# A graph attention layer on one core: four stages in place of five, head sums spread over six steps, and another order of the last steps

## The reference

```python
h = x @ W                                       # x: 8192 x 128
e = (h @ a1)[:, None] + (h @ a2)[None, :]
e = jnp.where(e > 0, e, 0.2 * e)
e = jnp.where(adj > 0, e, -9e15)                # adj: 8192 x 8192 int32, a one in 4096
attention = jax.nn.softmax(e, axis=1)
out = layernorm(x + elu(attention @ h))
```

## Time and profile before

| | us |
|---|---|
| median of 3 runs | 720.44 |
| lowest and highest | 719.63, 721.66 |
| the profiled execution | 721.3 |
| its span, first to last instruction | 719.5 |
| TensorE busy with products in it | 557.4 (77%) |
| ScalarE busy | 520.5 (72%) |
| VectorE busy | 480.7 (67%) |
| GpSimd busy | 443.6 (62%) |
| 285.57 MB moved, mean rate | 397 GB/s |

### The profile page before, as it was taken

One profiled execution on the slowest core, in us unless ns is written; L12 is line 12 of the kernel. 1 busy time (PEld: TensorE's weight loads), 2 busy tenths in 40 slices (PEclk: granted clock), 3 DMA queues, 4 the chain that ended last, 5 costly groups with the idle time before them and its releaser, 6 DMA issues.

```text
span 719.5 us, 11920 instructions
## 1 busy us (share of the span) xinstructions
PE 557.4 (77%) x3071; PEld 351.2 (49%) x3071; DVE 480.7 (67%) x2051; ACT 520.5 (72%) x414; POOL 443.6 (62%) x668
## 2 busy tenths in 40 slices
PE   0858799987778887778888787887778787777884
PEld 0323455554455554555455554554455554544583
DVE  1474777767766667667667667677766667667565
ACT  0847578787878777887878787878878777878511
POOL 2016267766766676676667676667666766777741
PEclk9987798899999999998889999799999999999957
DMA  9999999999999999999999999999999999999901
GB/s 353 326 422 422 384 413 429 427 422 425 428 425 429 426 426 429 425 427 425 428 426 427 427 428 427 428 426 426 428 425 428 429 427 428 426 423 424 284 17 31
DMA packets 34582, 285.57 MB, mean 397 GB/s; under 512 B 5512, under 2 KB 13856, under 8 KB 18048
## 3 DMA queue, kind: packets, MB, share of 16 engines
q1 hardware_dynamic: 29008, 276.83, 92.1%
q0 software_dynamic: 5120, 8.42, 3.3%
q10 hardware_dynamic: 432, 0.07, 0.1%
HBM read 283.18 MB, written 4.19 MB: 399 GB/s over the span
## 4 chain that ended last, share of the span: by engine, by line
DMA 63%; PE 12%; ACT 10%; DVE 6%; issue 5%; POOL 2%; SPq 0%; ACTq 0%; POOLq 0%; DVEq 0%
DMA adj_sb<-in_adj 60%; ACT adj_squared L551 10%; PE fold L653 7%; DMA a_sb<-in_L_gnn_a 2%; PE misc L678 2%; PE fold L649 1%; POOL edge_row L362 1%; PE x_att_ps L701 1%; DMA nb<-in_x,index 1%; DVE s_all L838 1%; PE small L668 1%; DVE x_times_wa L836 1%; DVE top_map L852 0%; DVE spread L374 0%; POOL nb L497 0%
## 5 line engine op out<-in xcount | busy, mean ns | idle before, releaser
L551 ACT ACTIVATE adj_squared<-adj_sb 128x4096 bf16<-128x4096 int32 x128 | 462.4, 3613 | 103.2 <-DMA adj_sb<-in_adj 97.2
L653 PE MATMUL fold<-adj_sb,bit_ident 128*128 128x512 bf16 x1024 | 302.0, 445 | 0.0
L497 POOL DMA_INDIRECT nb<-in_x,index x160 | 165.7, 1036 | 92.4 <-issue 64.2
L653 PEld LDWEIGHTS fold<-adj_sb,bit_ident 128*128 128x128 bf16 x1024 | 109.4, 107 | 150.6 <-issue 61.0
L649 PE MATMUL fold<-col_no,ident_bf 128*128 128x512 bf16 x128 | 53.2, 416 | 114.2 <-DMA adj_sb<-in_adj 101.7
L852 DVE MAX8 top_map<-fold 128x8 f32<-128x512 f32 x128 | 89.5, 699 | 67.1 <-PE fold L653 62.4
L362 POOL TENSOR_SCALAR edge_row<-row_iota,edge_in 128x128 f32<-128x128 int32 x186 | 129.4, 710 | 0.0
L378 POOL TENSOR_TENSOR spread<-edge_row,edge_w 128x384 f32<-128x384 f32 x60 | 51.9, 885 | 66.4 <-DVE edge_w L965 66.3
L477 POOL TENSOR_SCALAR empty_diag<-ident,counts 128x128 f32<-128x128 f32 x64 | 42.2, 665 | 68.5 <-DVE counts L889 35.4
L649 PEld LDWEIGHTS fold<-col_no,ident_bf 128*128 128x128 bf16 x128 | 16.4, 128 | 129.1 <-issue 101.4
L701 PEld LDWEIGHTS x_att_ps<-spread,nb 128*128 128x128 f32 x372 | 58.6, 225 | 9.8 <-issue 4.7
(11 more groups left out here) (120 smaller groups left out, 623.4 us busy)
## 6 DMA issues: line engine op xcount, KB each, us to landing
adj_sb<-in_adj SPq DMA_DIRECT2D x127, 2048.0 KB, 15.9
out<-x_sb SPq DMA_DIRECT2D x2, 1536.0 KB
nb<-in_x,index POOLq DMA_INDIRECT x160
adj_sb<-in_adj SPq DMA_DIRECT2D x2, 1024.0 KB, 15.1
out<-x_sb SPq DMA_DIRECT2D x5, 128.0 KB
out<-x_sb SPq DMA_DIRECT2D x1, 384.0 KB
W_sb<-in_L_gnn_W ACTq DMA_DIRECT2D x1, 64.0 KB, 7.9
x_sb<-in_x SPq DMA_DIRECT2D x4, 0.5 KB, 17.7
```

Source lines behind the costliest of these rows:

```text
L497: nc.gpsimd.indirect_dma_start(out=nb_of(j, g)[:, c, :], out_offset=None, in_=x[:, :], in_offset=bass.IndirectOffsetOnAxis(ap=index[:, g, ...
L551: nc.scalar.activation(adj_squared[:, h % 2, :], adj_sb[:, h % LOAD_SLOTS, :], ACT.Square, accum_out=half_sum[:, h:h + 1]).then_inc(square ...
L653: last = nc.tensor.matmul(fold[:, h % LOAD_SLOTS, :], bit_ident[:, b, :], adj_low[:, h % LOAD_SLOTS, b * FOLD:(b + 1) * FOLD, 0], start=Fa ...
```

## The change

The arithmetic is the same. On each engine work is written in another order:

- VectorE: `finish` is done for p3, behind `weights`, in place of p4 at the head of the step; `pick` of the first half comes ahead of `route`; `edge_weights` comes ahead of `lists` (except in the last step); in `lists` the count goes ahead of the cap.
- ScalarE: `copy_sums` comes behind the first square, `scale` (now for p4) behind the second, then `exp_weights` and `exp_elu`, all ahead of the third and fourth square.
- TensorE: `sum_neighbours` comes behind the first fold, ahead of `count_starts`; `times_W` ahead of the third fold.
- The head sums are made in eighths: four in step (0, 0), none in (0, 1), one in each of the four steps after that. TensorE's row sums are spread over three steps.
- The ending: VectorE does final's `indices` ahead of back1's `neighbour_scores`, and has no `finish(back3)` there, since that is now in the last step; ScalarE has no `scale(back4)` there. Final's five gathers have a semaphore each, for which its dot products wait one by one. SP waits for all five before its first store. Final's `sum_neighbours` starts when the spread of the first of its two tiles is done (`first_spread`).

The diff, whole but for a few lines of context:

```diff
         adj_sb = sb("adj_sb", [P, LOAD_SLOTS, HALF], i32)
         adj_low = adj_sb[:].bitcast(bf16).rearrange("p s (c two) -> p s c two", two=2)
         adj_squared = sb("adj_squared", [P, 2, HALF], bf16)
-        x_times_wa = sb("x_times_wa", [P, TILES // 4, D], fp32)
+        x_times_wa = sb("x_times_wa", [P, TILES // 8, D], fp32)
         ident = sb("ident", [P, P], fp32)
         bit_ident = sb("bit_ident", [P, BITS, P], bf16)
         ident_bf = sb("ident_bf", [P, P], bf16)
...
         weights_loaded = sem("weights_loaded")
         loaded = [sem(f"loaded{s}") for s in range(LOAD_SLOTS)]
         rest_loaded = sem("rest_loaded")
+        chunk_gathered = [sem(f"chunk_gathered{c}") for c in range(CHUNKS)]
+        first_spread = sem("first_spread")
         gathered = [sem(f"gathered{g}") for g in range(GROUPS)]
         out_stored = sem("out_stored")
         x_again = sem("x_again")
...
                     if eng is nc.vector:
                         last_one = eng.tensor_scalar(spread[:, t, k, :], edge_row[:, g, t, k, :], edge_w[:, c:c + 1],
                                                      None, ALU.mult)
+                if is_final(j, g) and t == 0:
+                    last_one.then_inc(first_spread, 1)
                 if eng is nc.gpsimd:
                     mine = edge_w[:, SPANS[t][0]:SPANS[t][0] + SPAN]
                     last_one = eng.tensor_tensor(spread[:, t, :, :], edge_row[:, g, t, :, :],
...
                 step(*back1)
                 step(*final)
+                for landed in chunk_gathered:
+                    sp.wait_ge(landed, 16)
                 for lo, hi in STORES:
                     sp.wait_ge(scaled, hi)
                     nc.sync.dma_start(out_tiles[:, lo * PAIR:hi * PAIR, :], x_sb[:, lo * PAIR:hi * PAIR, :]
...
                         nc.gpsimd.indirect_dma_start(
                             out=nb_of(j, g)[:, c, :], out_offset=None, in_=x[:, :],
                             in_offset=bass.IndirectOffsetOnAxis(ap=index[:, g, c:c + 1], axis=0),
-                            bounds_check=N - 1, oob_is_err=False).then_inc(gathered[g], 16)
+                            bounds_check=N - 1, oob_is_err=False).then_inc(
+                                chunk_gathered[c] if is_final(j, g) else gathered[g], 16)
                 def step(i, g):
                     p1, p2, p4 = (stage(i, g, k) for k in (1, 2, 4))
...
                     last.then_inc(scaled, 1)
                 def step(i, g):
-                    now, p2, p3, p5 = (stage(i, g, k) for k in (0, 2, 3, 5))
-                    if p5:
-                        scale(*p5)
+                    now, p2, p3, p4 = (stage(i, g, k) for k in (0, 2, 3, 4))
                     square_half(*now, 0)
-                    square_half(*now, 1)
-                    square_half(*now, 2)
                     if p3:
                         copy_sums(*p3)
+                    square_half(*now, 1)
+                    if p4:
+                        scale(*p4)
                     if p2:
                         exp_weights(*p2)
-                    square_half(*now, 3)
                     if p3:
                         exp_elu(*p3)
+                    square_half(*now, 2)
+                    square_half(*now, 3)
                 steps(act, step)
                 step(*back1)
                 step(*final)
-                scale(*back4)
                 exp_weights(*back1)
                 copy_sums(*back2)
                 exp_elu(*back2)
...
                 def sum_neighbours(j, g):
-                    pe.wait_ge(spread_ready, count(j, g))
+                    if is_final(j, g):
+                        pe.wait_ge(first_spread, 1)
+                    else:
+                        pe.wait_ge(spread_ready, count(j, g))
                     pe.wait_ge(diag_made, count(j, g))
                     if first(j) and g == 0:
                         pe.wait_ge(x_mean_ready, 1)
                     elif not is_final(j, g):
                         pe.wait_ge(x_att_ready, count(j, g) - 1)
                     for t in range(PAIR):
+                        if is_final(j, g) and t == 1:
+                            pe.wait_ge(spread_ready, count(j, g))
                         for k, c in enumerate(SPANS[t]):
                             nc.tensor.matmul(x_att_of(j, g)[:, t, 0:P], nb_of(j, g)[:, c, :], spread[:, t, k, :],
                                              start=k == 0, stop=False)
...
                 def step(i, g):
                     now, p1, p2, p3 = (stage(i, g, k) for k in range(4))
                     fold_half(*now, 0)
+                    if p3:
+                        sum_neighbours(*p3)
                     if p1:
                         count_starts(*p1)
                     fold_half(*now, 1)
-                    if p3:
-                        sum_neighbours(*p3)
                     if p1:
                         fill_edges(*p1)
                     if p2:
                         send_scores(*p2)
+                    if p3:
+                        times_W(*p3)
                     fold_half(*now, 2)
                     fold_half(*now, 3)
-                    if p3:
-                        times_W(*p3)
                     if p2:
                         send_shares(*p2)
-                    if first(i):
-                        sum_rows(g * TILES // GROUPS, (g + 1) * TILES // GROUPS)
+                    if first(i) and g == 0:
+                        sum_rows(0, TILES // 2)
+                    if first(i) and g == 1:
+                        sum_rows(TILES // 2, 3 * TILES // 4)
+                    if isinstance(i, int) and (i, g) == (1, 0):
+                        sum_rows(3 * TILES // 4, TILES)
                 def keep_warm(products, bank=3):
...
                 dve.wait_ge(wa_made, 1)
                 s.after(nc.vector.tensor_copy(wa_bc[:].rearrange("p k c -> p (k c)"), misc[:, P:3 * P]))
-                quarter = TILES // 4
+                eighth = TILES // 8
                 def own_scores(q):
-                    dve.wait_ge(x_loaded[q], 16)
-                    v.after(nc.vector.tensor_tensor(x_times_wa[:], x_sb[:, q * quarter:(q + 1) * quarter, :],
-                                                    wa_bc[:, 1:2, :].to_broadcast([P, quarter, D]), ALU.mult))
-                    v.after(nc.vector.reduce_sum(s_all[:, q * quarter:(q + 1) * quarter], x_times_wa[:], AX.X))
+                    dve.wait_ge(x_loaded[q // 2], 16)
+                    v.after(nc.vector.tensor_tensor(x_times_wa[:], x_sb[:, q * eighth:(q + 1) * eighth, :],
+                                                    wa_bc[:, 1:2, :].to_broadcast([P, eighth, D]), ALU.mult))
+                    v.after(nc.vector.reduce_sum(s_all[:, q * eighth:(q + 1) * eighth], x_times_wa[:], AX.X))
                 def mean_row():
                     dve.wait_ge(x_summed, 1)
...
                         dve.wait_ge(diag_made, count(j, g) - 1)
                         dve.wait_ge(tallied, count(j, g) - 1)
                     v.after(nc.vector.tensor_scalar(is_code[:], sent[:, :, 0:SLOTS], float(NO_CODE), None, ALU.is_gt))
+                    nc.vector.reduce_sum(found, is_code[:], AX.X).then_inc(listed, 1)
                     nc.vector.tensor_scalar(cap[:, g, :, :], is_code[:], 1e30, NEG, ALU.mult, ALU.add)
-                    nc.vector.reduce_sum(found, is_code[:], AX.X).then_inc(listed, 1)
                 def route(j, g):
...
                                             ALU.mult, ALU.add).then_inc(indexed, 1)
                 def neighbour_scores(j, g):
-                    dve.wait_ge(gathered[g], (j + 1) * (16 * CHUNKS))
+                    if not is_final(j, g):
+                        dve.wait_ge(gathered[g], (j + 1) * (16 * CHUNKS))
                     for c in range(CHUNKS):
+                        if is_final(j, g):
+                            dve.wait_ge(chunk_gathered[c], 16)
                         last = nc.vector.tensor_tensor_reduce(
                             out=dot[:, c, :], in0=nb_of(j, g)[:, c, :], in1=wa_bc[:, 0, :], scale=1.0, scalar=0.0,
                             op0=ALU.mult, op1=ALU.add, accum_out=t_edge[:, c:c + 1])
...
                     v = Steps(dve, v_step)
                 def step(i, g):
-                    now, p1, p2, p3, p4 = (stage(i, g, k) for k in range(5))
+                    now, p1, p2, p3 = (stage(i, g, k) for k in range(4))
                     fresh_steps()
-                    if p4:
-                        finish(*p4)
+                    pick(*now, 0)
                     if p1:
                         route(*p1)
                     if p2:
                         neighbour_scores(*p2)
-                    pick(*now, 0)
                     if p1:
                         indices(*p1)
                     pick(*now, 1)
                     if p2:
                         scores(*p2)
                         weights(*p2)
+                    if p3:
```

(16 more changed lines are left out.)

## The result

| | kernel before | kernel after |
|---|---|---|
| median | 721.29 us (719.63 to 721.84, 5 runs) | 727.33 us (724.22 to 728.45, 5 runs) |
| ratio | | 1.0084, 95% interval 1.0062 to 1.0105 |
| profiled execution | 721.3 us, span 719.5 | 724.22 us, span 722.4 |

The change makes the kernel 6 us slower, where 3.5 us less were forecast. So the mechanism can be read from it, but not its full size: no trace shows where the other 3 us went. The page of the kernel after: span, granted clock and GB/s in 40 slices, and the loads (KB, us to landing).

What follows compares the result with a forecast made beforehand. The prediction took the DMA stream of adjacency halves to bound the body, with an ending behind it. Terms -2.4 - 1.3 + 0.3 - 0.1 = -3.5 took the median from 720.44 to 716.9 us, with an 8-in-10 range of 714.4 to 719.4.

Steps and rivals of the forecast that it cites:

- Early gap: Stream dip at 84 to 92 us, behind head sums in step (0,1): spreading them closes it, -2.4 us.
- Body: Steps of four adjacency halves: later slots and VectorE's added eighths stay covered by the stream, 0 us.
- some 9 us: Steps 2 to 5: a slot must come free this much later than now before a gap forms.
- a time to landing below 8 us: Sign of being wrong: squares wait so long for scores that loads land less than 8 us after issue.
- Rival 2: Steps 2 to 5: the gap comes back as VectorE gets 2.3 us more in each; 719.3 us, chance 0.13.
- wait for the mean row: Part of the returning-gap rival: the mean row waits for TensorE's last row sums in step (1,0); no separate size.
- Last step: Behind the last loads: neighbour sums fill TensorE's idle time, last maximum at 673.2 instead of 674.60; taken as -1.3 us.
- neighbour sums before 662: Sign of being right, last step: TensorE's neighbour sums, behind the first fold, come before 662 us.
- Gather: Second-last stage's neighbour gather, issued earlier, shares the engines with the last half-load: +0.3 us, bounds 0 and 0.5.
- Ending: After the last half: indices ahead of dot products, held stores and finer waits save nothing on the path, 0 us.
- rival 3: Ending: TensorE regains full clock sooner, shares and second neighbour sums take 2.7 us less; 714.2 us, chance 0.10.
- rival 4: Ending: the held 3.5 MB of stores run slowly and become the end, near 743 us; chance 0.06.

Runs made afterwards that it cites:

- after_no_late_head: Kernel after without the four late eighths of the head sums (zeros in their place, for timing only): 720.88 us, ratio 0.9986.
- head_only: Kernel before with only the head sums spread in eighths over six steps and the row sums over three: 720.14 us, ratio 0.9988.
- after_weights_amid: Kernel after with VectorE's edge weights in the middle of the lists instead of ahead of them: 718.98 us, ratio 0.9982.
- after_eighth_mid: Kernel after with the four late eighths moved behind finish, ahead of the third maximum: 720.9 us, ratio 0.9995.
- after_act_late: Kernel after with ScalarE's exponentials put back behind the third square of the step: 726.3 us, ratio 1.0076.
- end_only: Kernel before with only the new ending (indices first, chunk-wise and tile-wise waits, held stores): 720.24 us, ratio 0.9994.
- head_end: Kernel before with the head sums spread over six steps and the new ending, order within steps as before: 719.95 us, ratio 0.9982.
- eighth_weights_amid: Kernel after with both edits: late eighths behind finish, edge weights in the middle of the lists: 719.37 us, ratio 0.9987.
- after_lists_first: Kernel after with VectorE's lists ahead of the edge weights again in every step: 725.56 us, ratio 1.0066.

## Why the prediction was wrong, point by point

- **Early gap, -2.4.** It closed as described (416 GB/s at 84 to 92 us). Alone it was worth 0.9 us of the median (0.9988), with an interval from a loss of 0.4 to a gain of 2.1: the term was sized too large.
- **Body, 0: the step that failed.** The text held 2.3 us per step against "some 9 us" that a slot may be late. Both numbers were fair (the eighth took 2.46; a load lands after 15.9 us in the kernel before and after 7.4 where the stream ran dry, 8.5 less, though the text's own 16 - 5 gives 11), the comparison was not: what a round is longer than the stream's step is lost again in each. At 82.5 us 12.7 - 7.4 = 5.3 us of the lead were left, and three rounds of 67.9 us in place of 60.6 took 7.3. Not all of it is the eighths': without them (after_no_late_head) the four steps took 23.4, 19.6, 18.5 and 21.7 us, with them 23.3, 21.2, 23.3 and 23.8. The forecast's own sign of being wrong, a time to landing below 8 us, came true, though its place of the gap (80 to 130 us) did not. I priced each edit by the wait it makes and never walked one whole round. What had lengthened it in the step shown: wait for the shares and edge weights 0.7 us (129.39 to 130.06), lists of 4.9 us (head_only: 3.2, from 123.96 to 127.15), the eighth 2.5, and TensorE first without work, then at half clock (how much this adds, no run separates).
- **Edge weights ahead of the lists.** I counted a wait of 1.3 us and 3 us of gain for GpSimd. That the spread would then run beside VectorE's lists was not seen, though it follows from the order. In the trace, from_base took 809 ns in the mean against 192. The Trainium skill has the rule (SBUF — State Buffer, SBUF: two separate sides): VectorE and GpSimd share a port pair as an exclusive lock, and a VectorE operation with two SBUF inputs waits for a whole GpSimd operation that reads SBUF and started first. The trace agrees: spread's two operations take 1.67 us, and from_base and lead end as the first and the second of them end. after_weights_amid takes away these 1.1 us a step together with the wait of 0.3 us for the shares, gives back 0.4 in is_code and cap, and the 7 us are gone; no run has one without the other. The four rounds got 8.6 us shorter, more than this accounts for. Nor is it a loss by itself: after_eighth_mid and after_no_late_head keep from_base at 808 and 809 ns and lose nothing. As far as the runs show, it costs only where the round also holds an eighth.
- **Rival 2** (the gap returns in steps 2 to 5) named the mechanism, with 719.3 us. Its size was wrong, by the same missing sum: it set the new gap at 2.4 us, as large as the old one, and 6.4 us of stream were missing. Its wait for the mean row was there too: TensorE's sums of step 3 waited 3.01 us for x_mean_bc, at 93.19 us, 0.51 without the eighths; but that step was as long without them (23.4 us), so this wait is not shown to have cost anything. "The margin of 9 us" was no argument against the rival as long as the lag could add up.
- **ScalarE.** Slots later by up to 6 us were forecast; loads land 2.9 us sooner after their issue, so slots came free about 3 us later. Putting the exponentials back (after_act_late) brings this to 14.9 us and gains nothing that the interval shows, so it is not what made the gap.
- **Last step, -1.3.** Not there. The last maximum is 2.75 us behind the last landing, before 2.5. The neighbour sums did leave their place ahead of fill_edges, and the second fold did run at full clock, as forecast (1.97 us for its eight products). But the first fold took 3.16 us and the third 3.02, both mostly at half clock:

```profile
661.22 3.16 PE L659 MATMUL fold<-adj_sb,bit_ident 128*128 128x512 bf16 x8
666.77 1.97 PE L659 MATMUL fold<-adj_sb,bit_ident 128*128 128x512 bf16 x8
669.12 1.40 PE L674 MATMUL small<-sent,row_edge 128*128 128x18 f32 x12 [0.38 <-DVE row_edge L917]
671.85 1.10 PE L724 MATMUL h_ps<-W_sb,x_att 128*128 128x128 f32 x4
673.16 3.02 PE L659 MATMUL fold<-adj_sb,bit_ident 128*128 128x512 bf16 x8
676.24 1.97 PE L659 MATMUL fold<-adj_sb,bit_ident 128*128 128x512 bf16 x7
678.35 0.70 DVE L867 MAX8 top_map<-fold 128x8 f32<-128x512 f32 x1 [1.25 <-PE fold L659]
```

  The step of the prediction that failed here is "neighbour sums before 662": behind the slow first fold they ended at 666.6. Allowing for the last landing, which came 3.5 us later than before, the second fold ends 0.8 us later than forecast, and the third starts 1.7 us later and takes 1.3 us longer. I counted only the idle time that the sums fill, not the one that they leave: in the body fill_edges then came behind 3.08 us without work and ran at half clock. In the last step that idle time is only 0.38 us, so why the third fold fell to half clock there is not shown.
- **Gather, +0.3.** The last loads land 16.0 us after their issue, before 16.2: no delay of it is seen.
- **Ending, 0.** Right as a sum (end_only 0.9994), and the dot products start at 688.05 without waiting for DMA. From the last maximum to the end it is 44.9 us before, 44.8 in end_only and head_end, and 44.05 after.
- **Clock in the ending (rival 3).** With the new order in the last steps the same ending took 43.3 us (eighth_weights_amid) to 48.5 (after_lists_first), with different clocks granted in it. Two stretches of the ending (PE busy time, PEclk, DMA share, GB/s), of after_no_late_head (47.1 us) and of the kernel after (44.05):

```profile
692.00:702.00 10.00, 8.74 (x37) 0.50 1.02 288
```
```profile
692.00:702.00 10.00, 8.48 (x48) 0.67 0.50 138
```

  So with the new order the ending varied by some 2 us to each side, and these two stretches go with the clock, which the sum did not have. The traces do not separate it from other causes. Whether that is what the four slower executions of the kernel after lost, no trace of them shows.
- **Held stores (rival 4).** They ran from 698 to 712 us where the forecast had 690 to 703, and did not become the end.

## What to carry to other kernels

Where a stream is kept full by a few slots, price an edit by the whole round that frees a slot, sum its links over all engines, and compare it with the stream's step: slack absorbs a shift once, an excess of the round comes again in each step. Work that must be done sometime belongs where its engine waits inside the round, not between two links of it: four eighths of 2.5 us cost some 7 us behind the lists and nothing that can be seen beside the folds. When an operation moves, look at what will then run beside it on an engine that shares its port, and at what idle time it leaves behind on the engine whose clock it kept up.

## What the runs showed of the hardware

VectorE's two-input operations of 32 elements took 0.19 us alone and 0.70 to 0.81 us beside GpSimd's spread of 128 x 384. Beside the same spread in after_weights_amid the eight-element maxima and replacements kept their 0.18 us, but is_code and cap, which read one tensor and a constant, took 0.47 and 0.42 us in the mean (0.30 and 0.19 in the kernel after):

```profile
L904 DVE TENSOR_SCALAR is_code<-sent 128x20 f32<-128x20 f32 x20 | 9.5, 473 | 2.4 <-DVE sent L899 2.0
L899 DVE MAX8 sent<-cand_rest 128x8 f32<-128x32 f32 x40 | 5.8, 186 | 0.7
```

So not only two-input operations got longer beside it. TensorE's granted clock from 200 to 600 us rose to 0.94 with added products, and the ratio rose from 1.0084 to 1.0129. ScalarE's wait for the scores was the largest wait in the kernel after, 116 us; moving its place in the order cut it to 27 us and left the time where it was.
